# Experts' gate and up products of a fused attention and mixture-of-experts layer: from three fp32r products against streamed weights to plain fp32 products with the weights stationary

## The reference, cut to what matters

```
logits = xt @ router_w.T + routing_bias
topk_p, topk_idx = top_k(sigmoid(logits), 2); topk_p = topk_p / sum(topk_p)
g = einsum('th,eih->tei', xt, wg);  u = einsum('th,eih->tei', xt, wu)
y = einsum('tei,ehi->teh', silu(g) * u, wd)
routed = einsum('te,teh->th', w, y)        # w: topk_p, scattered into (tokens, 8)
```

## Time and profile before

| | |
|---|---|
| three runs | 529.5, 529.93, 531.18 us, median 529.93 |
| profiled execution | 529.1 us, span 527.4 us, mean granted clock of PE 0.96 |
| PE busy over the span | 425.0 us, 81% |
| DVE, ACT, POOL busy | 405.1, 358.5, 328.2 us |
| first tile's transpose, last expert store | 91.4 us, 161.2 us |

### The profile page before, as it was taken

One profiled execution on the slowest core, in us unless ns is written; L12 is line 12 of the kernel. 1 busy time (PEld: TensorE's weight loads), 2 busy tenths in 40 slices (PEclk: granted clock), 3 DMA queues, 4 the chain that ended last, 5 costly groups with the idle time before them and its releaser, 6 DMA issues.

```text
span 527.4 us, 11888 instructions
## 1 busy us (share of the span) xinstructions
PE 425.0 (81%) x2857; PEld 310.8 (59%) x2857; DVE 405.1 (77%) x1466; ACT 358.5 (68%) x1092; POOL 328.2 (62%) x492
## 2 busy tenths in 40 slices
PE   0657243999997889979988996998899699899885
PEld 0555121677775667657656764765676476567663
DVE  3854713666652899888988988998898899889885
ACT  1334123566666878968886895888689688768864
POOL 2275778940002789678867957876795887777140
PEclk9999767899999999989998999999899999989999
DMA  7940111222221000000001000000100000010010
GB/s 219 350 134 32 45 45 59 56 75 79 78 68 32 1 12 11 2 21 22 0 0 30 10 0 20 20 0 0 34 6 0 20 20 0 0 35 5 2 42 10
DMA packets 28159, 21.04 MB, mean 40 GB/s; under 512 B 3512, under 2 KB 25312, under 8 KB 28000
## 3 DMA queue, kind: packets, MB, share of 16 engines
q1 hardware_dynamic: 25264, 16.46, 10.5%
q0 software_dynamic: 2048, 4.20, 2.7%
q10 hardware_dynamic: 816, 0.03, 0.1%
HBM read 12.41 MB, written 8.26 MB: 39 GB/s over the span
## 4 chain that ended last, share of the span: by engine, by line
POOL 31%; PE 21%; issue 20%; DVE 15%; DMA 5%; ACT 4%; POOLq 1%; SPq 1%; DVEq 1%; ACTq 0%
POOL rnorm L415 6%; POOL slot_x L405 6%; POOL arena_b L495 6%; POOL rpow L418 5%; PE bank L1140 4%; PE bank L930 3%; DVE arena_b L885 3%; DVE arena_b L869 3%; POOL pnull L484 3%; PE bank L932 3%; PE bank L931 3%; DMA arena_b<-in_L_ffn_wu_dram 2%; DMA arena_b<-slot_x 2%; PE bank L1072 2%; DVE ssq L846 2%
## 5 line engine op out<-in xcount | busy, mean ns | idle before, releaser
L649 ACT ACTIVATE arena_b<-arena_b,nmx 128x130 f32<-128x130 f32 (+1 forms) x256 | 115.2, 458 | 29.5 <-DVE nmx L885 20.5
L869 DVE TENSOR_SCALAR arena_b<-arena_b,rden 128x130 f32<-128x130 f32 (+1 forms) x256 | 103.9, 450 | 4.5
L885 DVE CUSTOM_DVE_ANT_0 arena_b<-bank,bias 128x130 f32<-128x130 f32 (+1 forms) x256 | 80.9, 353 | 17.1 <-PE bank L1072 9.3
L1072 PE MATMUL bank<-arena_a 64*128 64x130 f32 (+1 forms) x512 | 59.8, 352 | 23.6 <-DVE nmx L885 22.8
L418 POOL TENSOR_TENSOR rpow<-ssm,mhalf 128x8 f32<-128x8 f32 x32 | 52.7, 1648 | 40.4 <-DVE ssm L850 40.4
L1063 PE MATMUL bank<-ident,arena_b 128*128 128x128 f32 x384 | 67.2, 284 | 7.1 <-DVE arena_b L869 7.1
L431 POOL TENSOR_TENSOR arena_b<-arena_b,rnorm 128x512 f32<-128x512 f32 x64 | 67.1, 1048 | 8.4 <-POOL rnorm L421 3.8
L587 ACT ACTIVATE arena_b<-bank 128x512 f32<-128x512 f32 x64 | 38.2, 597 | 31.3 <-PE bank L932 30.5
L415 POOL TENSOR_TENSOR rnorm<-ssm,mhalf 128x8 f32<-128x8 f32 x32 | 52.4, 1639 | 7.7 <-DVE ssm L850 7.7
L846 DVE TENSOR_REDUCE ssq<-arena_b 128x8 f32<-128x512 f32 x64 | 43.4, 678 | 15.5 <-ACT arena_b L587 15.2
L1072 PEld LDWEIGHTS bank<-arena_a 64*128 64x128 f32 x512 | 33.6, 186 | 36.4 <-DVE nmx L885 30.4
(11 more groups left out here) (209 smaller groups left out, 1111.7 us busy)
## 6 DMA issues: line engine op xcount, KB each, us to landing
slot_x<-probT SPq DMA_DIRECT2D x3, 832.0 KB, 9.8
arena_b<-slot_x SPq DMA_DIRECT2D x39, 64.0 KB, 1.9
slot_y<-arena_b SPq DMA_DIRECT2D x39, 64.0 KB, 1.5
arena_b<-in_L_ffn_wd_dram SPq DMA_DIRECT2D x1, 1024.0 KB, 9.4
arena_b<-in_L_attn_Wkv_dram SPq DMA_DIRECT2D x1, 1024.0 KB, 8.6
arena_b<-in_L_attn_x_dram SPq DMA_DIRECT2D x8, 128.0 KB, 2.1
out_dram<-arena_b SPq DMA_DIRECT2D x8, 128.0 KB, 1.8
arena_b<-in_L_attn_Wq_dram SPq DMA_DIRECT2D x1, 512.0 KB, 6.5
```

Source lines behind the costliest of these rows:

```text
L649: sc.activation(prob[:, h % 4, c], sim[h % 2][:, c], ACT.Exp, scale=-1.0, bias=nmx[:, h % HEADS, t:t + 1], accum_out=den[:, h % HEADS, t:t ...
L869: ve.tensor_scalar(pr, pr, rden[:, h % HEADS, t:t + 1], None, ALU.mult).then_inc(g.pn, 1)
L885: ve.tensor_tensor_reduce(out=sim[h % 2][:, c], in0=bank[h % 2][:, c], in1=bias[:, c], scale=-SLOPES[h], scalar=3e38, op0=ALU.add, op1=ALU ...
L1072: ins = te.matmul(bank[half][:, c0:c1], qT[r, h // 2, q0:q0 + P], kT[r, h // 2, 0:c1 - c0], start=True, stop=True)
```

## The change

The experts' weights `egu` are kept once, in plain fp32: in the setup ACT copies each group out of PSUM and DVE has no part in it. In the experts' loop SP loads the tile's expert number into a register of its own, and a DMA inside SBUF copies that expert's 128 x 512 gate and up weights (256 KB) into a ring `mw` of 5 buffers; the first five are issued before the scatter ends. PE loads the four 128 x 128 blocks of `mw` as stationary weights and streams the 128 transposed tokens past each, in plain fp32, so that gate and up come out with the inner width on the partitions. The transposes of h, their copy `mhT` and the subtraction for the tokens' low part fall away. The last product follows gate and up by two steps in place of three, and SP stores at a lag of 6. The PSUM ring for gate and up has 4 banks in place of 2. Cut to its core:

```diff
+RG, RW = 4, 5
-        egu = [sb("egu_hi", [P, E, 2 * I], F32R), sb("egu_lo", [P, E, 2 * I], F32R)]
+        egu = sb("egu", [P, E, 2 * I])
+        mw = [sb(f"mw{i}", [P, 2 * I]) for i in range(RW)]
...
@@ SP @@
+            def weights(n):
+                e = sync.value_load(tile_expert[0:1, bass.ds(n, 1)], min_val=0, max_val=E - 1)
+                if n >= RW:
+                    sync.wait_ge(g.m_gups, n - RW + 1)
+                sync.dma_start(mw[n % RW][:], egu[:, bass.ds(e, 1), :].rearrange("p o n -> p (o n)")
+                               ).then_inc(m_w[n % RW], 16)
+
+            sync.wait_ge(g.slots_ready, 2)
+            sync.wait_ge(g.w_gu, E)
+            for n in range(RW):
+                weights(n)
             sync.wait_ge(g.scattered, 16 * NT * TOPK)
...
-                for st in range(SLOT_TILES + 7):
+                for st in range(SLOT_TILES + 6):
                     n = staged(st, 0)
                     if n is not None:
                         if n >= RX:
                             sync.wait_ge(g.m_xps, n - RX + 1)
                         sync.dma_start(mx_in[n % RX][:], xg_dram[n * P:(n + 1) * P, :]).then_inc(m_in[n % RX], 16)
-                    n = staged(st, 7)
+                        if n >= RW:
+                            weights(n)
+                    n = staged(st, 6)
                     if n is not None:
                         sync.wait_ge(g.m_yev, n + 1)
...
@@ ACT, setup @@
+                if what == "gu":
+                    act.wait_ge(g.w_ps, n + 1)
+                    sc.activation(dst[0], bank[n % EARLY][:, 0:w], ACT.Copy).then_inc(g.w_gu, 1)
+                    return
...
@@ PE, one step, behind the transpose of tile st @@
                     n = staged(st, 4)
                     if n is not None:
                         pe.wait_ge(g.m_h, n + 1)
                         if n >= 2:
-                            pe.wait_ge(g.m_hT, n - 1)
-                        for c in range(2):
-                            ins = te.transpose(bank[4 + n % 2][:, c * P:(c + 1) * P], mh[n % RH][:, c * P:(c + 1) * P], ident[:])
-                        ins.then_inc(g.m_hps, 1)
-                    n = staged(st, 2)
-                    if n is not None:
-                        pe.wait_ge(g.m_xlo, n + 1)
-                        if n >= 2:
-                            pe.wait_ge(g.m_h, n - 1)
-                        w = [t[:, bass.ds(e_of[n], 1), :].rearrange("p o n -> p (o n)") for t in egu]
-                        three(bank[2 + n % 2][:], mxT[n % RH], w, True, True).then_inc(g.m_gups, 1)
-                        if n + 1 < SLOT_TILES:
-                            e_of[n + 1] = expert_of(n + 1)
-                    n = staged(st, 5)
-                    if n is not None:
-                        pe.wait_ge(g.m_hT, n + 1)
-                        if n >= 2:
                             pe.wait_ge(g.m_yev, n - 1)
                         w = ed[:, bass.ds(e_of[n], 1), :].rearrange("p o n -> p (o n)")
                         for c in range(2):
                             cc = slice(c * P, (c + 1) * P)
-                            ins = te.matmul(bank[6 + n % 2][:, 0:DIM], mhT[n % 2][:, cc], w[:, cc], start=c == 0, stop=c == 1)
+                            ins = te.matmul(bank[6 + n % 2][:, 0:DIM], mh[n % RH][:, cc], w[:, cc], start=c == 0, stop=c == 1)
                         ins.then_inc(g.m_yps, 1)
+                    n = staged(st, 2)
+                    if n is not None:
+                        pe.wait_ge(g.m_xev, n + 1)
+                        if n >= RG:
+                            pe.wait_ge(g.m_h, n - RG + 1)
+                        pe.wait_ge(m_w[n % RW], 16 * (n // RW + 1))
+                        for k in range(4):
+                            kk = slice(k * P, (k + 1) * P)
+                            ins = te.matmul(bank[2 + n % RG][:, kk], mw[n % RW][:, kk], mxT[n % RH][:], start=True, stop=True)
+                        ins.then_inc(g.m_gups, 1)
+                        if n + 1 < SLOT_TILES:
+                            e_of[n + 1] = expert_of(n + 1)
```

More of the change, by code:

```diff
@@ L108, in build @@
         my = [carve(DIM) for _ in range(RY)]
+        mxT = [carve(P) for _ in range(RH)]
         at[0] = loop_from
@@ L129, in build @@
         xs1, xs2 = ([carve_r(SEQ), carve_r(SEQ)] for _ in range(2))
-        mxT = [[carve_r(P), carve_r(P)] for _ in range(RH)]
-        mhT = [sb(f"mhT{i}", [P, I]) for i in range(2)]
         rt[0] = 4 * SEQ
@@ L205, in build @@
         block = ctx.enter_context(nc.Block())
+        m_w = [sem(f"m_w{r}") for r in range(RW)]
         m_in = [sem(f"m_in{r}") for r in range(RX)]
@@ L295, in build @@
         groups = [([raw_gu[:, w, 2 * e + c, :] for w in range(2) for c in range(2)],
-                   [t[:, e, :] for t in egu], "gu") for e in range(E)]
+                   [egu[:, e, :]], "gu") for e in range(E)]
         groups += [([raw_d[:, e, c * P:(c + 1) * P] for e in (e2, e2 + 1) for c in range(2)],
@@ L306, in splits, with group_out @@
             return sum(1 for _, dst, _ in groups[:n] if len(dst) == 2)
+        def group_out(eng, n):
+            if n < E:
+                eng.wait_ge(g.w_gu, n + 1)
+            else:
+                eng.wait_ge(g.w_lo, n - E + 1)
         def settled(eng):
@@ L529, in split_group @@
             def split_group(n):
-                srcs, dst, _ = groups[n]
+                srcs, dst, what = groups[n]
+                w = len(srcs) * P
+                if what == "gu":
+                    act.wait_ge(g.w_ps, n + 1)
+                    sc.activation(dst[0], bank[n % EARLY][:, 0:w], ACT.Copy).then_inc(g.w_gu, 1)
+                    return
                 if len(dst) == 1:
                     return
-                w = len(srcs) * P
                 act.wait_ge(g.w_ps, n + 1)
@@ L656, in experts @@
             def experts():
-                for st in range(SLOT_TILES + 6):
-                    n = staged(st, 6)
+                for st in range(SLOT_TILES + 5):
+                    n = staged(st, 5)
                     if n is not None:
@@ L668, in experts @@
                             act.wait_ge(g.m_gups, n - RH + 1)
[L669 to L675 removed]
+                        sc.activation(mxT[n % RH], bank[n % 2][:, 0:P], ACT.Copy).then_inc(g.m_xev, 1)
                     n = staged(st, 2)
@@ L680, in experts @@
                             act.wait_ge(g.m_ga, n - 1)
-                        sc.activation(mth[n % 2], bank[2 + n % 2][:, 0:I], ACT.Tanh, scale=0.5).then_inc(g.m_th, 1)
+                        sc.activation(mth[n % 2], bank[2 + n % RG][:, 0:I], ACT.Tanh, scale=0.5).then_inc(g.m_th, 1)
             experts()
@@ L892, in experts @@
             def experts():
-                for st in range(SLOT_TILES + 2):
-                    n = staged(st, 0)
-                    if n is not None:
[L896 to L900, removed]
-                    n = staged(st, 2)
[L902 to L911, removed]
+                for n in range(SLOT_TILES):
+                    ps = bank[2 + n % RG]
+                    dve.wait_ge(g.m_th, n + 1)
+                    ve.scalar_tensor_tensor(out=mga[n % 2], in0=mth[n % 2], scalar=1.0, in1=ps[:, 0:I],
+                                            op0=ALU.add, op1=ALU.mult).then_inc(g.m_ga, 1)
+                    dve.wait_ge(g.m_ga, n + 1)
+                    if n >= RH:
+                        dve.wait_ge(g.m_yps, n - RH + 1)
+                    ve.scalar_tensor_tensor(out=mh[n % RH], in0=mga[n % 2], scalar=0.5, in1=ps[:, I:2 * I],
+                                            op0=ALU.mult, op1=ALU.mult).then_inc(g.m_h, 1)
             experts()
@@ L940, in transpose_group @@
                 if n >= EARLY:
-                    pe.wait_ge(g.w_lo, n - EARLY + 1)
+                    group_out(pe, n - EARLY)
                 for i, src in enumerate(srcs):
@@ L994, in _ @@
                 transpose_group(n)
-            pe.wait_ge(g.w_lo, len(groups))
+            pe.wait_ge(g.w_gu, E)
+            pe.wait_ge(g.w_lo, len(groups) - E)
             pe.wait_ge(g.wraw_lo, 3)
@@ L1107, in experts @@
                 e_of = {0: expert_of(0)}
-                for st in range(SLOT_TILES + 5):
+                for st in range(SLOT_TILES + 4):
                     n = staged(st, 0)
```

10 lines of the change are left out of this document (3 added, 7 removed).

## The result

The changed kernel took 556.65, 554.13 and 555.64 us in three runs and the kernel before, in four runs beside them, 529.81 us in the median: a ratio of 1.0471, with a 95% interval of 1.0436 to 1.0506. (A fourth run of the changed kernel, which had a mean granted clock of 0.67, took 614.63 us and is left out of the ratio.) The forecast was 539.5 us with a range of 533 to 549: slower as forecast, but the loss is 26 us where 9.6 were expected, and the range did not hold it. The profiled execution took 556.65 us with a span of 554.9 us and a mean granted clock of 0.95.

A forecast was written before the change was run, and what follows sets the result against it. SP's queue was taken to bound the experts' loop at 2.05 us a step: 98.8 + 63.6 + 8.7 puts attention's start at 171.0 against 161.3 us, +9.7. Forecast 539.5 us, range 533 to 549.

The forecast's parts named there:

- the store's issue: SP's queue, each expert step: 0.37 us from the start of the store's issue to the tile load's.
- 31 steps: Experts' loop: loads of tiles 8 to 38 follow at SP's pace, 31 x 2.05 = 63.6 us.
- tail: From the last tile load to attention: landing, PE's last steps, tanh, DVE operations, last product, copy and queue, 8.7 us.
- The copy's own issue: SP's queue, each step: the weights' DMA inside SBUF with its gap, 0.42 us, between 0.36 and 0.47.
- The register load: SP's queue, each step: register load with range operation and assert, 0.64 us, between 0.47 and 0.84.
- The rival by which it costs 0.50: SP's queue: register load dear at 0.50 us, step 2.25 us, +16 us, 546 us; chance 0.10.
- the clock rival: PE in the experts' loop: clock falls, step 2.86 us, +25 us and more, 555 us; chance 0.05.
- PE's step: PE in the experts' loop: 13 passes of 0.11 us, 1.43 us against 1.61, the queue wait vanishing.
- The loop through the store: Experts' loop: tile load, PE, tanh, copy, store, next load take 4.65 us for three steps, 1.55 each.
- The first rival: Experts' loop: SP's queue does not bind, the 1.55 us loop holds, -5.8 us, 524 us; chance 0.10.
- Setup: Before the scatter: DVE's L732 no longer waits for four subtractions, starts at 20.05 instead of 21.01, gaining 0.96 us.
- The DMA engines: Experts' loop: transfers take together 1.3 us of the 2.05 us step, so they are hidden.

The follow-up runs named there:

- e2: The kernel before plus SP's register load and 256 KB copy per tile into two unread buffers, other engines unchanged: 555.68 us, ratio 1.0485 to the kernel before.
- e8: Changed kernel with stores issued by ACT, odd tiles' weight copies from tile 7 by POOL, six weight buffers: 525.12 us, ratio 0.9927 to the kernel before.
- e3: Changed kernel with each tile's expert number fixed in the program, so no register load, same bytes copied: 534.65 us, ratio 1.008 to the kernel before.
- e4: Changed kernel with each tile's store issued from ACT's queue behind its tanh instead of SP's: 547.39 us, ratio 1.032 to the kernel before.
- e10: Changed kernel with the weight copy issued behind the store instead of between load and store: 563.69 us in one run, 28.6 above the kernel before.
- e6: Changed kernel with weight copies of 128 x 128 instead of 128 x 512 from tile 5 on: 550.92 us in one run.
- e9: Changed kernel with the register load kept but the copy's address fixed in the program: 559.65 us in one run, 24.6 above the kernel before.
- e5: Changed kernel without weight copies of tiles 5 to 38, and SP's store lag 7 instead of 6: 524.49 us, ratio 0.9912 to the kernel before.
- e1: Changed kernel without the weight copies of tiles 5 to 38, PE's part kept: 531.21 us, ratio 1.0016 to the kernel before.

## Why the prediction was wrong

**The mechanism was right.** SP's queue binds; e2 gives the loss without PE's part, e8 takes it away without taking out any work. What failed is the size of SP's step, 2.05 us where 2.48 were measured, and in it above all the store's issue. By its own steps, with the medians of L345, L361, L367 and L342 and their gaps:

| term | forecast, us | measured, us |
|---|---|---|
| first load of tile 7 | 98.8 | 98.5 |
| store's issue to load's | 0.37 | 0.63 |
| tile load | 0.47 | 0.49 |
| register load, range, assert | 0.64 | 0.71 |
| address | 0.15 | 0.10 |
| weights' DMA with its gap | 0.42 | 0.54 |
| step | 2.05 | 2.48 |
| 31 steps | 63.6 | 79.0 |
| tail | 8.7 | 10.6 |
| attention starts | 171.0 | 188.1 |

- **The store's issue is the step that failed.** It was taken over from the kernel before with "0.37", as a row in hand, and had no bounds. But that row shows a store issued after idle time: the load's issue of 106.99 ends at 107.42, 0.82 us ahead of the next store at 108.24 (the 1.25 us that the prediction calls idle hold the load's own 0.43). The change took the idle time away and put a copy inside SBUF in front; e3 shows 0.32 and 0.59 in one kernel, e4 and e10 that whatever follows the copy pays, and e6 that a copy of a quarter of the bytes asks as much. +0.26 us in each of 31 steps is 8.1 of the 17.1 us by which attention starts later than forecast; with an upper end for it, the step's own would have been 2.56 and not 2.30. The prediction had a hint in the earlier trace rows itself: the tile load's issue takes 0.333 us at the shortest, but 0.43 in the median, right behind the store's.
- **The copy's own issue** was bounded by 0.36 and 0.47 and took 0.54 with its gap: 3.7 us. No row of before held such a DMA, and the bounds from the nearest rows were too narrow; e9 puts 0.03 of it on the address in a register.
- **The register load** was near, +0.07 us (2.2), and the address 0.05 less (-1.6). Its own duration differs with its place: 0.27 in e6 and e10, 0.42, 0.55 in e4. The rival by which it costs 0.50 was off by 0.08. The floor of some 0.6 us that the Trainium skill gives for it ("DMA: Bandwidth & Descriptors", "Latency and other measured facts") isn't borne out: in the changed kernel SP's shortest is 0.263 us, its median 0.419.
- **31 steps are not 31 medians.** 31 x 2.48 is 76.9, and 79.0 passed: the first two steps took 3.01 and 2.73 us, and one took 3.8, with this in it (timeline of SP):

```profile
172.74 0.50 SPq L345 DMA_DIRECT2D mw<-egu  x1
173.28 1.91 SPq L367 DMA_DIRECT2D slot_y<-arena_b  x1
175.24 0.43 SPq L361 DMA_DIRECT2D arena_b<-slot_x  x1
```

  Such issues have a companion that no experiment here tests. Over the twelve traces SP has 38 DMA issues of more than 0.8 us between 97 and 180 us, and 37 of them start within 0.85 us of a packet of 16 KB on a DMA queue that the view calls `q8`, kind "instruction". For the one above it lies between 173 and 174 us:

```profile
q8 instruction: 1, 0.02, 9.1%
```

  The same holds of 48 of the 53 tile loads that took more than 2.8 us to land: such a packet started during the landing or up to 1.3 us ahead of the load's issue. The kernel before has these packets too, but SP has slack there.

- **The tail** took 1.9 us more. The last steps' chain:

```profile
178.61 1.71 PE bank L1147 x8
182.89 0.89 PE bank L1147 x8
188.10 0.65 PE bank L1032 x4
```

The first eight passes take 1.71 us, those of a later step 0.89. The window that holds the first has a granted clock of 0.72, those around it 1.00:

```profile
155.00:176.00 21.00, 14.87 (x108) 12.64 (x106) 6.86 (x17) 7.08 (x26) 0.00 (x0) 1.00 0.46 151
176.00:182.00 6.00, 4.53 (x24) 4.38 (x25) 1.55 (x4) 1.00 (x5) 0.00 (x0) 0.72 0.43 141
```

So for a part of it PE had the lower of its two levels (1.2 GHz), after it had waited 2.06 us for the tile behind the long store. That is the clock rival in small, at one place; over the stretch the clock was 0.98, so the rival itself, a step of 2.86 us throughout, is wrong, although its 555 us were nearest to the result. Its 555 are wrong besides: by the prediction's own sum, 98.8 + 31 x 2.86 + 8.7, attention would start 35 us later and the time be 565; the 25 us are only what it adds to SP's 2.05.

**PE's step.** The passes of 0.11 us are confirmed, and the wait for PE's queue all but went. The step is 1.53 and not 1.43 where PE binds (e5), by 0.1 us between transpose and product. The loop through the store, forecast at 1.55, measures 1.62 in e1 when nothing else is on SP. The first rival took this for a gain of 6 us; e1 shows none. What the sum missed there is that a closed loop keeps each late landing, so its mean (1.74) is above its median. e5, with the loop opened, comes to the rival's 524 us.

**Setup.** `xn1` is at 19.86 us where 20.05 was forecast:

```profile
19.86 2.36 DVE L754 TENSOR_TENSOR arena_a<-arena_a,rstd 128x1024 f32<-128x1024 f32 x2 [2.52 <-POOL rstd L411]
```

```profile
L427 POOL DMA_INDIRECT slot_x<-arena_a,slot x32: 954/966/3027, 42.6 to 86.7; - x32
```

The scatter starts 1.1 us earlier, but its last DMA only 0.6 us. That is no more than these times vary between runs: in e2, which keeps the subtractions, `xn1` is at 20.26 us and the last scatter at 86.2. So a gain of 0.96 in the time is not shown.

**The DMA engines** were rightly costed as hidden: share 0.45, landing 2.1 us in place of 1.9; e3 and e8 pass the same bytes in 1.81 and 1.57 us a step in the mean.

**What stays open.** What SP's queue is held by in the 0.63 us behind a copy inside SBUF; whether the packets on `q8` cause the long issues and late landings or only come with them; what sets the register load's duration between 0.27 and 0.55 us. Two variants weren't tried: weights used by PE straight from `egu`, with the register in the address of the stationary operand, and the register load put between the copy and the next DMA. If it kept its 0.71 us there, the next DMA would start late enough to take 0.32 us, as in e3; that would save up to 0.27 of the 2.48 us, an estimate from these rows.

## What to carry to other kernels

A ring of buffers covers a transfer's delay and not the rate of the queue that issues it: sum the issuing queue's instructions per step, and share them out over engines with slack before anything else (here 556 to 525 us). What an issue costs depends on what stands ahead of it; a row read where the queue was idle is a lower bound once the queue is full, and such a term needs an upper end too. Where a load waits behind a store that needs the result of an earlier load, count that loop, and give the store one step more than the sum asks for, since a closed loop keeps every stall.

## What the runs showed of the hardware

- The issue of a 64 KB DMA on SP's queue took 0.32 us after idle time, 0.43 to 0.46 right behind another such DMA to or from DRAM, and 0.59 right behind a copy inside SBUF, of 256 KB or of 64 KB (e6), with or without a register load in the step (e3). In e3 the 0.59 shrank by as much as the issue started later, down to 0.32. The copy's own issue took 0.47 us with a fixed address and 0.50 with one in a register.
- Loading a register took SP 0.42 us behind the tile load in the changed kernel, 0.55 behind a tile load of 0.59 us (e4), 0.27 with small copies (e6) and with full ones behind the store (e10), and POOL 0.33 (e8); the whole operation with range and assert cost SP 0.71 us.
- POOL issued the same 256 KB copy in 0.59 us, between its arithmetic operations (e8).
- 37 of 38 DMA issues of SP above 0.8 us started within 0.85 us of a 16 KB packet of kind "instruction"; the cause is not shown.
- A plain fp32 product of 128 x 128 by 128 columns was two passes of 0.11 us at a granted clock of 1.00, for gate and up from the ring as for the last product with `ed`. Four of them took 0.89 us; the three fp32r products of 512 columns started 0.23 us apart in the kernel before.
